# Four-network GNN kernel on one Trainium2 core: where ScalarE issues its transfers of P in the edge MLP of network L1

## The chip, the core and the metric

The kernel runs on one NeuronCore of a Trainium2 chip, as one launch. The metric is the device time of the launch in microseconds (us). The program uses all five instruction streams of the core: TensorE (PE), VectorE (DVE), ScalarE (ACT), GpSimd (POOL) and SyncE (SP). ScalarE and SyncE both issue direct DMA transfers, GpSimd issues indirect ones (gathers).

## The reference

Four small graph networks run one after another on 3125 nodes with 16 features and 103125 edges; each adds its output to `x` and normalises. The change lies in the second, L1, which has four layers with 128 hidden features. One layer is, cut to the part that matters:

```python
for i in range(L):                                   # L = 4
    ef = jnp.concatenate([h[row], h[col], edge_attr], axis=1)
    ef = jax.nn.silu(ef @ edge_w1[i] + edge_b1[i])
    ef = jax.nn.silu(ef @ edge_w2[i] + edge_b2[i])
    ef = ef * edge_mask
    agg = jax.ops.segment_sum(ef, row, num_segments=n)
    ...                                              # node MLP, h = h + nf
```

So every edge needs a row of `h` for its one end, a row for its other end, a two-layer MLP with silu, and a sum over the edges of a node.

## The kernel before

The first product of the edge MLP is split: per layer, `P = h @ w1[0:128]` and `Q = h @ w1[128:256]` are worked out for all nodes and written to the tables `p_tab` (three bf16 parts of 128 values each, 768 bytes a row) and `q_tab` (f32) in HBM. The edges lie sorted in 840 tiles of 128 edges. Three tiles are a group (M3 = 3), so a layer has G3 = 280 groups of 384 edges. `edge_mlp` (from line 1436) runs them; it is called once per layer, four times in all.

Every engine runs its own list of steps, one step per group, and the lists are tied by counting semaphores. `turns` (line 927) makes the list: eight steps, one for each slot h = 0 to 7 of the ring buffers (U3 = 8), are a turn; K3 = 35 turns are a layer, of which the first two and the last are written out and the 32 between are a loop. In the step of group n:

- TensorE: `first` (lines 1523 to 1531) adds up z1 of group n in PSUM: edge features (L1523), nine bf16 products of the P rows in `pb` with a one-hot matrix `oht` (L1526), in three groups of four a product of `qb` (L1528), and two or three transposes of the gathered Q rows `qg` (L1531). Then `sums` (L1549) adds the messages of group n-2 to the node sums; it waits for `m_seed`. Then `second` (L1540) multiplies h1 of group n-1 by w2 into z2.
- ScalarE: `two` (L1595), the silu of z2 of group n-2, which waits for `m_z2`; then `one` (L1588), the silu of z1 of group n, which waits for `m_z1`; and in even steps `fetch`, below.
- VectorE: `seed` (L1622) writes the bias b2 over z2, once `two` has read it, and so releases `sums` and `second`; then one-hot matrices (L1632, L1633, L1641) and the indices for the gathers (L1617).
- GpSimd: two or three gathers of Q rows (L1480) for a group five steps on.
- SyncE: in even steps all that a pair of groups needs besides: places, near, edge features, `qb`, and the three transfers of P rows of the even group (L1503).

There is only one z2 in PSUM. So `second` of a group can't start before `seed` has followed `two` of the group before it, and `two` can't start before `second` has ended.

ScalarE's `fetch(k, h)` is called at the end of even steps for the pair six steps on. It waits on `m_z1` for its ring slot, loads four numbers from `at_p` into registers (`address`, line 961, a TENSOR_LOAD), and issues three transfers of 96 KB each (L1581) of P rows into `pb` for the pair's odd group. All of it stands in ScalarE's list between `one` of the even step and `two` of the odd step. Its transfers are first read by `first` seven steps later.

Of the kernel before, what the change touches and what calls it, by code (L numbers as in the profile page):

```python
# [13 lines left out]
P = 128  # L14
N, FIN = 3125, 16
E = 103125
NB = -(-N // P)
# [8 lines left out]
M3 = 3  # L26
U3 = 8
# [27 lines left out]
def gnn_kernel(nc, a, out):  # L55

    with ExitStack() as ctx:
        def sb(name, shape, dt=F32, st=None):
            return (st or ctx).enter_context(nc.sbuf_tensor(name, shape, dt))

        def dram(name, shape, dt=F32):
            return nc.dram_tensor(name, shape, dt, kind="Internal").ap()

        def sem(name):
            return ctx.enter_context(nc.semaphore(name))
# [43 lines left out]
        p_tab = dram("p_tab", [NP, 3 * HID], BF16)  # L109
# [455 lines left out]
        at_p = sb("at_p", [1, G3, 4], I32)  # L565
# [361 lines left out]
        def turns(eng, step, rounds=K, ring=U):  # L927

            for k in (0, 1):
                for h in range(ring):  # L930
                    step(k, h)
            with eng.Fori(2, rounds - 1) as k:
                for h in range(ring):
                    step(k, h)
            for h in range(ring):
                step(rounds - 1, h)
# [24 lines left out]
        def address(eng, row, top):  # L961

            _, at = nc.values_load_multi_w_load_instructions(
                row, engines=[eng], min_val=0, max_val=top,
                skip_runtime_bounds_check_because="worked out on the chip from counts that are bounded by the shapes")
            return at
# [391 lines left out]
        with ExitStack() as st:  # L1358
# [5 lines left out]
            h = sb("h", [P, NB, FIN], F32, st)  # L1364
# [67 lines left out]
        m_pl, m_sp, m_act = ([sem(f"m_{n}{q}") for q in range(U3 // 2)] for n in ("pl", "sp", "act"))  # L1432
        Z1, Z2 = 3584, NP

        def edge_mlp(layer, we36, w2, b1, b2):
# [4 lines left out]
            def here(k, h, lag=0):  # L1440
                return not isinstance(k, int) or lag <= k * U3 + h < G3
# [7 lines left out]
            def moved(k, h, by):  # L1449

                d, slot = divmod(h + by, U3)
                return (k + d if d else k), slot

            with ExitStack() as st:
                qidx = sb(f"qidx{layer}", [P, U3, M3], I32, st)
                qg = sb(f"qg{layer}", [P, U3, M3, HID], F32, st)
                pb = sb(f"pb{layer}", [P, U3, M3, 3 * HID], BF16, st)
# [11 lines left out]
                with nc.Block() as block:  # L1469
                    @block.gpsimd  # L1470
                    def _(pool):
                        def gather(k, h):
                            n = k * U3 + h
                            if here(k, h, U3):

                                pool.wait_ge(m_z1, g0 + n - U3 + 1)
                            pool.wait_ge(m_idx, g0 + n + 1)
                            pool_gate(pool)
                            for j in range(gathered(h)):
                                pool.indirect_dma_start(qg[:, h, j, :], None, q_tab,  # L1480
                                                        IndirectOffsetOnAxis(ap=qidx[:, h, j:j + 1], axis=0)).then_inc(m_got[h], 16)
                        turns(pool, gather, K3, U3)
# [87 lines left out]

                    @block.scalar
                    def _(act):
                        def fetch(k, h):
                            q, n = h // 2, k * U3 + h
                            if not here(k, h):
                                return
                            if here(k, h, U3):
                                act.wait_ge(m_z1, g0 + n - U3 + 2)
                            at = address(mybir.EngineType.Activation, at_p[0:1, bass.ds(n + 1, 1), 0:4].rearrange("a g j -> a (g j)"), (NB - 1) * P)
                            for j in range(M3):  # L1580
                                act.dma_start(pb[:, h + 1, j, :], p_tab[bass.ds(at[j], P), :]).then_inc(m_act[q], 16)  # L1581

                        def one(k, h):
                            n = k * U3 + h
                            if here(k, h, 2):
                                act.wait_ge(m_z2, g0 + n - 1)
                            act.wait_ge(m_z1, g0 + n + 1)
                            act.activation(h1[:, h % 2, :], z1, ACT.Silu, bias=b1).then_inc(m_h1, 1)  # L1588

                        def two(k, h):  # L1590
                            n = k * U3 + h
                            if here(k, h, 2):
                                act.wait_ge(m_sum, g0 + n - 1)
                            act.wait_ge(m_z2, g0 + n + 1)
                            act.activation(h2[:, h % 2, :, :], z2.rearrange("p (j f) -> p j f", j=M3), ACT.Silu).then_inc(m_h2, 1)  # L1595

                        def step(k, h):
                            if here(k, h, 2):
                                two(*moved(k, h, -2))
                            one(k, h)  # L1600
                            if h % 2 == 0:
                                fetch(*moved(k, h, 6))
                        for h in (0, 2, 4):
                            fetch(0, h)
                        turns(act, step, K3, U3)
                        two(K3 - 1, U3 - 2)
                        two(K3 - 1, U3 - 1)
# [376 lines left out]
```

## Time and profile before

| what | value |
|---|---|
| median of 3 runs | 8916.31 us (8913.84 to 8923.95) |
| the profiled execution's own time | 8926.24 us |
| its span in the trace | 8924.5 us |
| mean granted clock of TensorE over the span | 0.794 of full speed |
| busy: TensorE, weight loads, VectorE, ScalarE, GpSimd | 6479.8, 5299.9, 4955.1, 2834.7, 5094.9 us |

The profile gives the busy time of each engine, the span in slices with the granted clock and the DMA share, groups of instructions by source line with the idle time of the engine in front of them, the waits between engines, and a timeline. In the timeline the "ACTq" and "SPq" rows are the issuing of transfers by ScalarE and SyncE; they don't count as busy. The ends of matmuls are modelled. The four layers' edge MLPs lie in the trace at about 2364 to 3285, 3370 to 4282, 4367 to 5289 and 5373 to 6289 us.

### The profile page before, as it was taken

Reading aid. Unit: us, or ns where it says so; the run is one execution under the profiler, and the core shown is the slowest. Engines: PE = TensorE matmul, PEld = TensorE weight load, DVE = VectorE, ACT = ScalarE, POOL = GpSimd, SP = SyncE. Lnnn points to the kernel's source line nnn. Section 1 sums busy time; section 2 is a strip of 40 time slices with the busy share of each in tenths; the row PEclk is TensorE's granted clock in tenths of the full one; section 3 lists DMA queues with packets and bytes.
Section 4 is the critical chain, followed back from the end, with each engine's and each line's share of the span. In section 5 each row is a group of like instructions: output and inputs, shape, how many; then the busy total and the mean of one; then the engine's idle time right before and its main releaser. Section 6 shows DMA issues by size and latency. Waiting matters only on the chain. (4 is left out here: it accounts for less than half of the span.)

```text
span 8924.5 us, 233638 instructions
## 1 busy us (share of the span) xinstructions
PE 6479.8 (73%) x55142; PEld 5299.9 (59%) x55143; DVE 4955.1 (56%) x13861; ACT 2834.7 (32%) x8499; POOL 5094.9 (57%) x7138
## 2 busy tenths in 40 slices
PE   1222225767688878888788878888866666888998
PEld 1111114555477756777577756777455555787998
DVE  6333346867455545555455545555322222998999
ACT  1222203545233333333233333333133333222554
POOL 3777736756366646666366646666067776222554
PEclk8555555555799999999899999999655555999999
DMA  2000004434477757777577757777311000332232
GB/s 63 3 3 3 3 29 133 121 98 120 126 200 200 200 132 206 202 203 199 134 201 202 201 132 203 202 203 199 88 24 7 7 7 6 79 82 59 73 72 60
DMA packets 1320021, 1000.55 MB, mean 112 GB/s; under 512 B 479878, under 2 KB 1224219, under 8 KB 1319000
## 3 DMA queue, kind: packets, MB, share of 16 engines
q1 hardware_dynamic: 942230, 649.30, 26.7%
q0 software_dynamic: 134272, 178.98, 10.4%
q10 hardware_dynamic: 243392, 170.76, 6.6%
q8 instruction: 57, 0.93, 0.0%
q14 instruction: 70, 0.57, 0.0%
HBM read 951.88 MB, written 54.19 MB: 113 GB/s over the span
## 5 line engine op out<-in xcount | busy, mean ns | idle before, releaser
L1480 POOL DMA_INDIRECT qg<-q_tab,qidx x2520 | 2390.0, 948 | 1376.2 <-issue 769.9
L1622 DVE COPY ps<-b 128x384 f32<-128x384 f32 x1120 | 627.9, 561 | 1693.5 <-ACT h L1595 1655.3
L1067 PE MATMUL ps<-rhs_i,ohi 128*128 128x128 f32 (+2 forms) x8640 | 1216.7, 267 | 209.1 <-issue 197.1
L1549 PE MATMUL ps<-ohm,h 128*128 128x128 f32 x6720 | 1034.1, 291 | 380.7 <-DVE ps L1622 371.4
L1067 PEld LDWEIGHTS ps<-rhs_i,ohi 128*128 128x128 f32 (+1 forms) x8640 | 1000.4, 163 | 339.1 <-issue 280.6
L1549 PEld LDWEIGHTS ps<-ohm,h 128*128 128x128 f32 x6720 | 839.3, 192 | 592.0 <-issue 591.7
L1595 ACT ACTIVATE h<-ps 128x384 f32<-128x384 f32 x1120 | 549.2, 490 | 1824.7 <-PE ps L1540 1744.8
L1033 POOL COPY near<-x 128x48 bf16 x2160 | 675.4, 351 | 790.7 <-PE ps L1056 433.8
L1195 POOL DMA_INDIRECT got_m<-y_tab,idx_m x832 | 813.1, 977 | 473.5 <-issue 252.3
L375 POOL DMA_INDIRECT list_by_src<-ring,rpos x808 | 782.9, 969 | 348.9 <-issue 255.0
L1212 PE MATMUL ps<-rhs_m,ohi_m 128*128 x2880 | 668.8, 403 | 413.1 <-ACT rhs_m L1238 387.7
L1641 DVE TENSOR_SCALAR ohm<-iota_row,loc_p,w_p 128x128 f32<-128x128 f32 x3360 | 961.1, 358 | 0.0
L1540 PE MATMUL ps<-w,h 128*128 128x128 f32 x6720 | 943.4, 277 | 0.0
L1128 DVE TENSOR_TENSOR ohi<-iota_row,dst_i 128x512 f32<-128x512 f32 (+1 forms) x1080 | 930.5, 862 | 0.0
L1212 PEld LDWEIGHTS ps<-rhs_m,ohi_m 128*128 128x128 f32 x2880 | 637.0, 328 | 445.7 <-issue 445.5
L1588 ACT ACTIVATE h<-ps,b 128x384 f32<-128x384 f32 x1120 | 650.1, 580 | 707.5 <-PE ps L1531 666.4
L1540 PEld LDWEIGHTS ps<-w,h 128*128 128x128 f32 x6720 | 850.3, 194 | 0.0
L1526 PE MATMUL ps<-oht,pb 128*128 128x128 bf16 x10080 | 766.2, 222 | 0.0
L1252 DVE TENSOR_TENSOR ohi_m<-iota_row,dst_i 128x512 f32<-128x512 f32 x360 | 249.3, 693 | 831.3 <-PE ps L1212 827.3
L1526 PEld LDWEIGHTS ps<-oht,pb 128*128 128x128 bf16 x10080 | 572.3, 98 | 197.1 <-issue 197.1
L1123 DVE TENSOR_SCALAR oht_i<-places_i,iota_p 128x512 bf16<-128x512 bf16 (+1 forms) x1080 | 512.8, 475 | 177.8 <-PE ps L1067 160.2
L1031 POOL COPY near<-z 128x384 bf16 x720 | 344.8, 508 | 366.8 <-PE ps L1056 305.0
(443 smaller groups left out, 8613.0 us busy)
## 6 DMA issues: line engine op xcount, KB each, us to landing
pb<-p_tab ACTq DMA_DIRECT2D x1680, 96.0 KB
pb<-p_tab SPq DMA_DIRECT2D x1680, 96.0 KB
places<-place_by_turn SPq DMA_DIRECT2D x560, 192.0 KB
places_i<-place_by_meeting SPq DMA_DIRECT2D x360, 256.0 KB, 3.4
places_i<-place_by_meeting SPq DMA_DIRECT2D x720, 128.0 KB, 3.1
qb<-q_tab SPq DMA_DIRECT2D x840, 64.0 KB
qg<-q_tab,qidx POOLq DMA_INDIRECT x2520
nears<-near_by_turn SPq DMA_DIRECT2D x560, 64.0 KB
```

The source lines that it names most:

```text
L375: pool.indirect_dma_start(list_s[:, :], IndirectOffsetOnAxis(ap=rpos[:, h, c:c + 1], axis=0), ring[:, h, c, :], None).then_inc(scattered[h ...
L1033: m = pool.tensor_copy(near[:, h, j, :], table[:, bass.ds(at[j], 48)])
L1067: m = pe.matmul(ps[:, bass.ds(to[j], width)], ohi[:, h, j, :], rhs[:, h, j, 0:width], start=False, stop=True, skip_group_check=True)
L1128: dve.tensor_tensor(ohi[:, h, :, :], iota_row[:, None, :].to_broadcast([P, M, P]), dst_i[:, bass.ds(n * M, M)][:, :, None].to_broadcast([P ...
L1195: pool.indirect_dma_start(got[:, h, j, :], None, y_tab, IndirectOffsetOnAxis(ap=idx[:, h, j:j + 1], axis=0)).then_inc(d_got[h], 16)
L1212: m = pe.matmul(ps[:, bass.ds(to[j], 32)], ohi[:, h, j, :], rhs[:, bass.ds(at[j], 1), :].rearrange("p t f -> p (t f)"), start=False, stop= ...
L1480: pool.indirect_dma_start(qg[:, h, j, :], None, q_tab, IndirectOffsetOnAxis(ap=qidx[:, h, j:j + 1], axis=0)).then_inc(m_got[h], 16)
L1526: pe.matmul(z1[:, j * P:(j + 1) * P], pb[:, h, j, q_ * HID:(q_ + 1) * HID], oht[:, h, j * P:(j + 1) * P], start=False, stop=False)
L1540: m = pe.matmul(z2[:, j * P:(j + 1) * P], h1[:, h % 2, j * P:(j + 1) * P], w2, start=False, stop=True, skip_group_check=True)
L1549: m = pe.matmul(ps[:, bass.ds(to[M3 * (h % 2) + j], P)], h2[:, h % 2, j, :], ohm[:, h % 2, j, :], start=False, stop=True, skip_group_check ...
L1588: act.activation(h1[:, h % 2, :], z1, ACT.Silu, bias=b1).then_inc(m_h1, 1)
L1641: m = dve.tensor_scalar(ohm[:, h % 2, j, :], iota_row[:, :], loc_p[:, bass.ds(t, 1)], w_p[:, bass.ds(t, 1)], ALU.is_equal, ALU.mult)
```

## The change

`fetch` is cut in two: `find(k, h)` waits for the ring slot and loads the four numbers; `fetch(k, h, j)` issues one of the three transfers. In an even step `find` now stands between `two` and `one`, and transfer 0 behind `one`. In the odd step that follows, transfer 1 stands between `two` and `one`, and transfer 2 behind `one`. The three fetches ahead of the first step stay as they were.

```diff
-                        def fetch(k, h):
-                            q, n = h // 2, k * U3 + h
+                        at = []
+
+                        def find(k, h):
+                            n = k * U3 + h
                             if not here(k, h):
                                 return
                             if here(k, h, U3):
                                 act.wait_ge(m_z1, g0 + n - U3 + 2)
-                            at = address(mybir.EngineType.Activation, at_p[0:1, bass.ds(n + 1, 1), 0:4].rearrange("a g j -> a (g j)"), (NB - 1) * P)
-                            for j in range(M3):
-                                act.dma_start(pb[:, h + 1, j, :], p_tab[bass.ds(at[j], P), :]).then_inc(m_act[q], 16)
+                            at[:] = address(mybir.EngineType.Activation, at_p[0:1, bass.ds(n + 1, 1), 0:4].rearrange("a g j -> a (g j)"), (NB - 1) * P)
+
+                        def fetch(k, h, j):
+                            if not here(k, h):
+                                return
+                            act.dma_start(pb[:, h + 1, j, :], p_tab[bass.ds(at[j], P), :]).then_inc(m_act[h // 2], 16)
...
                         def step(k, h):
                             if here(k, h, 2):
                                 two(*moved(k, h, -2))
+                            if h % 2 == 0:
+                                find(*moved(k, h, 6))
+                            else:
+                                fetch(*moved(k, h, 5), 1)
                             one(k, h)
                             if h % 2 == 0:
-                                fetch(*moved(k, h, 6))
+                                fetch(*moved(k, h, 6), 0)
+                            else:
+                                fetch(*moved(k, h, 5), 2)
                         for h in (0, 2, 4):
-                            fetch(0, h)
+                            find(0, h)
+                            for j in range(M3):
+                                fetch(0, h, j)
```

On ScalarE, inside the loop of a layer, a pair of steps before (L1595 is `two`, L1588 is `one`, the TENSOR_LOAD is the address load, ISA and REGISTER_ALU are its sequencer's register work):

```order
L1595 ACTIVATE h<-ps 128x384 [waits m_z2,m_sum]
L1587 REGISTER_ALU [waits m_z2]
L1588 ACTIVATE h<-ps,b 128x384 [waits m_z1]
L1578 ISA
L963 ISA [waits m_z1]
L963 TENSOR_LOAD at_p
L1581 ISA
L1581 DMA pb<-p_tab 128x384
L1581 ISA
L1581 DMA pb<-p_tab 128x384
L1581 ISA
L1581 DMA pb<-p_tab 128x384
```

Here one load and three transfers stand in a row between `one` and the next `two`. The same place after the change (L1600 is `two`, L1593 is `one`, L1586 the transfers):

```order
L1600 ACTIVATE h<-ps 128x384 [waits m_z2,m_sum]
L1580 ISA
L963 ISA [waits m_z1]
L963 TENSOR_LOAD at_p
L1592 REGISTER_ALU [waits m_z2]
L1593 ACTIVATE h<-ps,b 128x384 [waits m_z1]
L1586 ISA
L1586 DMA pb<-p_tab 128x384
```

and the odd step behind it:

```order
L1600 ACTIVATE h<-ps 128x384 [waits m_z2,m_sum]
L1586 ISA
L1586 DMA pb<-p_tab 128x384
L1592 REGISTER_ALU [waits m_z2]
L1593 ACTIVATE h<-ps,b 128x384 [waits m_z1]
L1586 ISA
L1586 DMA pb<-p_tab 128x384
```

In front of each `two` and each `one` there is now at most one transfer or one load. The instructions of TensorE, VectorE, GpSimd and SyncE and their waits stand in the same order as before.

## Rows read from the trace of the kernel before

**Rows 1.** Groups by line over the whole span: busy, mean ns, idle before.
```profile
L1549 PE MATMUL ps<-ohm,h 128*128 128x128 f32 x6720 | 1034.1, 291 | 380.7 <-DVE ps L1622 371.4
```

**Rows 2.** Waits in 3400 to 4200 us: total us, times, longest.
```profile
DVE ps L1622 <- ACT h L1595: 357.3, 248, 2.2
...
POOL qg L1480 <- DVE qidx L1617: 101.6, 78, 2.0
...
PE ps L1549 <- DVE ps L1622: 72.4, 124, 0.9
```

**Rows 3.** Timeline, first matmul of each group in a turn of layer 1: start, length.
```profile
3500.90 0.33 PE L1523 MATMUL ps<-eat,we 36*128 36x384 bf16 x1 [0.34 <-issue]
...
3503.61 0.33 PE L1523 MATMUL ps<-eat,we 36*128 36x384 bf16 x1
...
3507.28 0.33 PE L1523 MATMUL ps<-eat,we 36*128 36x384 bf16 x1
...
3510.19 0.33 PE L1523 MATMUL ps<-eat,we 36*128 36x384 bf16 x1
...
3513.60 0.33 PE L1523 MATMUL ps<-eat,we 36*128 36x384 bf16 x1
...
3519.91 0.33 PE L1523 MATMUL ps<-eat,we 36*128 36x384 bf16 x1
...
3522.83 0.33 PE L1523 MATMUL ps<-eat,we 36*128 36x384 bf16 x1
...
3526.58 0.33 PE L1523 MATMUL ps<-eat,we 36*128 36x384 bf16 x1 [0.31 <-issue]
```

**Rows 4.** Timeline of slots 2 and 3 of that turn, ScalarE and what it releases.
```profile
3507.44 0.49 ACT L1595 ACTIVATE h<-ps 128x384 f32<-128x384 f32 x1 [1.78 <-PE ps L1540]
...
3507.96 0.56 DVE L1622 COPY ps<-b 128x384 f32<-128x384 f32 x1 [1.10 <-ACT h L1595]
...
3508.66 0.93 PE L1549 MATMUL ps<-ohm,h 128*128 128x128 f32 x6
...
3508.75 0.58 ACT L1588 ACTIVATE h<-ps,b 128x384 f32<-128x384 f32 x1 [0.82 <-PE ps L1531]
...
3509.41 1.33 ACTq L1581 DMA_DIRECT2D pb<-p_tab  x3
3509.42 0.83 PE L1540 MATMUL ps<-w,h 128*128 128x128 f32 x6
...
3510.85 0.49 ACT L1595 ACTIVATE h<-ps 128x384 f32<-128x384 f32 x1 [1.52 <-PE ps L1540]
...
3511.37 0.56 DVE L1622 COPY ps<-b 128x384 f32<-128x384 f32 x1 [1.79 <-ACT h L1595]
3511.50 0.58 ACT L1588 ACTIVATE h<-ps,b 128x384 f32<-128x384 f32 x1 [0.16 <-PE ps L1531]
...
3512.07 0.93 PE L1549 MATMUL ps<-ohm,h 128*128 128x128 f32 x6 [0.60 <-DVE ps L1622]
```

**Rows 5.** Timeline ahead of layer 0: nine transfers and three loads in a row.
```profile
2355.66 5.22 ACTq L1581 DMA_DIRECT2D pb<-p_tab  x9
```

**Rows 6.** Timeline, first matmul of three groups in layer 0.
```profile
2814.76 0.33 PE L1523 MATMUL ps<-eat,we 36*128 36x384 bf16 x1
...
2817.78 0.33 PE L1523 MATMUL ps<-eat,we 36*128 36x384 bf16 x1
...
2821.20 0.33 PE L1523 MATMUL ps<-eat,we 36*128 36x384 bf16 x1
```

**Rows 7.** Timeline of GpSimd, a gather in an unbroken row of them.
```profile
3562.26 0.94 POOL L1480 DMA_INDIRECT qg<-q_tab,qidx  x1 [0.30 <-issue]
```

**Rows 8.** Two stretches: busy of each engine, granted clock, DMA share, GB/s.
```profile
3500.00:4100.00 600.00, 537.63 (x4807) 447.46 (x4806) 330.76 (x1258) 199.62 (x373) 398.00 (x419) 1.00 0.75 202
3366.00:3376.00 10.00, 3.92 (x25) 2.87 (x25) 2.83 (x12) 0.58 (x1) 7.56 (x9) 0.62 1.04 275
```

## Prediction

> **What bounds the kernel now.** I began with the groups by line. In the whole span TensorE sat idle for 380.7 us in front of L1549, `sums`, and 371.4 us of that ended with VectorE's L1622, `seed` [rows 1]. The waits of layer 1 give the link behind it: `seed` in turn waited 248 times for ScalarE's L1595, `two`, and TensorE waited 124 times for `seed`, 72.4 us in 800 us [rows 2]. There are some 249 groups in that stretch, so only every second group makes TensorE wait. No wait on a transfer stands in the list.
>
> The timeline says which. The first matmuls of the groups of one turn [rows 3] start 2.71, 3.67, 2.91, 3.41 us after one another in slots 0 to 3; the pair of slots 4 and 5 takes 6.31, slot 6 takes 2.92 and slot 7 takes 3.75, with the 0.31 us of TensorE's loop end in it. The turn is 25.68 us. Even steps are short, odd steps long. In the even slot 2 [rows 4] ScalarE starts `one` at 3508.75. Its three issues then take it from 3509.41 to 3510.74. Meanwhile `second` ends on TensorE at 3509.42 + 0.83 = 3510.25. `two` starts at 3510.85, right behind the issues, and not at 3510.35, where it would follow `second` as closely as it does elsewhere (0.10 us). `seed` is late with it, and `sums` stalls 0.60 us. One step before, with no issue in front of it, `two` started at 3507.44 and `sums` had no idle time at all. So the path that sets the end here is `second`, `two`, `seed`, `sums`, `second`, through four engines' queues, and ScalarE's issues lie on it once a pair.
>
> **What the freed path would take.** From rows 4: `sums` to `second` 0.76 us (3508.66 to 3509.42), `second` 0.83, to `two` 0.10, to `seed` 0.52 (3510.85 to 3511.37), `seed` 0.56, to `sums` 0.14. That is 2.91 us, the length of slots 2 and 6 [rows 3]. The chain, not TensorE's own work, already sets the even steps; TensorE's own work for a group is the 2.71 us of slot 0, which has the loop end in front of it as a cushion.
>
> **The change, part by part.**
> *Removed from behind `one` of the even step:* the load and two of three issues. An issue is 1.33 / 3 = 0.44 us [rows 4]. The batch held ScalarE from 3508.75 to 3510.85, 2.10 us; with one issue instead of three that is 2.10 - 0.89 = 1.21 us, even if the load's share stayed in it. `two` is needed 1.60 us after the start of `one` (3508.75 to 3510.35). So transfer 0 is hidden by TensorE's `second`, with 0.39 us to spare, and the lateness of 0.50 us goes.
> *Added between `two` and `one` of the even step:* wait and load. The wait is for a z1 that TensorE finished a step earlier, so it costs nothing. The load: nine issues and the two loads between them took 5.22 us [rows 5], so a load is at most (5.22 - 9 x 0.44) / 2 = 0.63 us; the lower bound is nothing. From `two` at 3507.44 to `one` at 3508.75 there are 1.31 us, and `two` itself takes 0.49 [rows 4]. 0.49 + 0.63 = 1.12 fits. If this cover were gone, `one` would slip, and nobody needs h1 before the next group's `first`, at 3510.19, while `one` ended at 3509.33: another 0.86 us of slack. I take nothing.
> *Added between `two` and `one` of the odd step:* transfer 1. `two` 0.49, a gap as before the issues now of under 0.10, 0.44 for the issue, and 0.11 until ScalarE starts the next activation (3510.74 to 3510.85): 1.14 of 1.31 us. Nothing.
> *Added behind `one` of the odd step:* transfer 2, 1.21 us of 1.60 as above. Nothing. At slot 7 ScalarE's branch comes on top, but there `sums` of slot 0 has the loop end's cushion.
> *The transfers themselves:* the same 288 KB in the same queue, the last of them issued about one step (3 us) later than before. They are read seven steps on, some 20 us, so they don't come late by that. SyncE's and GpSimd's lists are untouched.
>
> **The sum.** Every odd step falls to the chain's 2.91: slot 1 saves 3.67 - 2.91 = 0.76, slot 3 saves 3.41 - 2.91 = 0.50, slot 5 saves 6.31 - 2 x 2.91 = 0.49. Slot 7 keeps its loop end; I take 0.45, a little under the others. 2.20 us a turn, 25.68 to 23.5. Layers 1 to 3 look alike: 105 turns, 231 us. In layer 0 a plain step takes 3.02 us and a pair 6.44 [rows 6], so a pair saves 0.40; four pairs, 35 turns, 56 us. Together 287 us. The profiled execution took 8926.24 us, so 8639 for one like it; it lies 10 us above the median of 8916.31, from which 287 us gives **8629 us**. A difference of 0.2% (18 us) is about what a measurement of this kernel can tell from none.
>
> The bounds: if all layers fall to 23.4 to 23.5 and the starts and ends of layers gain too, the saving nears the 371.4 us less what slots 3 and 7 keep (about 0.1 us each, since their `first` is shorter than the chain; 28 us), 340 us: 8575; I don't think the starts gain, so 8588 is the low end. If every layer's chain is as slow as layer 0's, 140 x 1.6 = 224 us: 8692.
>
> **A rule against it.** The issue of three transfers holds ScalarE 1.33 us, and `two` is late by 0.50 for it [rows 4]. The Trainium skill, "DMA: Bandwidth & Descriptors", section "Issuing engines are not separate DMA queues", says that issuing from several engines saves only the sequencer's time for it, and calls that usually small beside the transfer. By that rule there is little to win by moving an issue. The trace disagrees here, since the sequencer's time lies in front of an activation on the path.
>
> **The rivals.**
> *A, GpSimd becomes the bound.* A turn has 18 gathers, each 0.94 + 0.30 us apart when nothing holds them [rows 7]: 22.3 us, against 23.5 forecast. It fits, by 5%; it waits for VectorE's indices now, 101.6 us in 800 [rows 2], so it has slack. But should each of the eight groups add 0.2 us between its gathers, it would need 24.0; then the gain is 1.7 x 140 less layer 0's share, some 225 us: 8690. Chance 0.08.
> *B, the transfers come late.* The DMA share is 0.75 at 202 GB/s [rows 8]. At 23.5 us a turn it would be 0.82 at 221 GB/s. Against: the engines moved 275 GB/s at the start of layer 1 [rows 8], and nothing waits for a transfer now. For: near a full share queues grow. If half the gain went to this: 8916 - 143 = 8773. Chance 0.09.
> *C, no change.* Either `two` was late for another reason than the issues, with 0.11 us between the two a coincidence, or the issue time is as small as the skill's rule has it. It stays at 8916. Chance 0.04.
> *D, slower: a lone issue costs ScalarE nearly what three do.* The place is behind `one`, in every step now and not in every second. If the 2.10 us that ScalarE was held were set-up and not number, `two` would be 0.50 late in all eight steps of a turn: 4.0 us, where now 2.2 are lost. 1.8 x 140 = 250 us more: 9166. It decides from a hold of 1.60 us on, and the kernel gets slower from about 1.88 us. Against it: nine issues took 5.22 us and three 1.33, so the price goes with the number. Chance 0.04.
>
> **How the numbers follow.** The forecast has the rest, 0.75. The range from 8588 to 8700 takes in the forecast's bounds and rival A; B, C and D, 0.17 together, are left out. Faster by over 0.2%: the forecast, A and B, 0.92. Same: C, 0.04. Slower: D, 0.04.
>
> **What would show it.** In the profile after, the first matmuls of layer 1 should stand 2.9 us apart in odd and even steps alike, a turn at 23.5 us; `two` should start 0.1 us behind the end of `second` in every step; TensorE's idle time in front of `sums` should fall from 380.7 us to under 90. The wait of `one` for z1 should stay, as the sign that load and transfer 1 fit in front of it. GpSimd's wait for the indices should shrink to near 1 us a turn, and the DMA share rise to 0.82. The prediction is wrong if `two` starts right behind an issue in any slot (D), if the gathers run without a wait for indices while TensorE waits for them at L1531 (A), or if TensorE waits for transfers (B).

## The result

The changed kernel takes 8633.99 us (median of 4 runs, 8630.37 to 8649.17), the kernel before 8916.33 us in the same comparison: a ratio of 0.9685, 95% interval 0.9668 to 0.9702, 282 us less. The forecast was 8629 us.

| what | before | after |
|---|---|---|
| the profiled execution's own time | 8926.24 us | 8636.00 us |
| its span | 8924.5 us | 8634.3 us |
| busy: TensorE, VectorE, ScalarE, GpSimd | 6479.8, 4955.1, 2834.7, 5094.9 us | 6448.2, 4984.1, 2837.3, 5094.3 us |
| mean granted clock over the span | 0.794 | 0.787 |

### The profile after

The same work is done (the busy times are alike) in 290 us less. The page's groups by line, as in [rows 1]; L1635 is `seed` in the changed kernel:

```profile
L1549 PE MATMUL ps<-ohm,h 128*128 128x128 f32 x6720 | 1033.9, 291 | 61.4 <-DVE ps L1635 30.9
```

TensorE's idle time in front of `sums` fell from 380.7 us [rows 1] to 61.4, and what ended on `seed` from 371.4 to 30.9. That is 319 us, more than the gain, since other idle time of TensorE grew: in front of L1523, the first matmul of a group, from 68.2 to 108.4 us, and in front of L1531, which reads the gathered rows, from nothing to 17.2 us, all of it ended by a gather's landing. What was added lies in the last turns of the layers, shown below.

The waits of 3350 to 4100 us, to be read against [rows 2]:

```profile
ACT h L1593 <- PE ps L1531: 200.2, 238, 1.3
...
POOL qg L1480 <- DVE qidx L1630: 46.4, 98, 2.0
```

TensorE's wait for `seed` is down to one of 0.2 us in this stretch. `one` (L1593) waits for z1 in nearly every step: ScalarE is early there, behind the load and behind transfer 1 alike.

The first matmuls of one turn of layer 1, the counterpart of [rows 3]:

```profile
3427.52 0.33 PE L1523 MATMUL ps<-eat,we 36*128 36x384 bf16 x1 [0.35 <-issue]
...
3430.22 0.33 PE L1523 MATMUL ps<-eat,we 36*128 36x384 bf16 x1
...
3433.08 0.33 PE L1523 MATMUL ps<-eat,we 36*128 36x384 bf16 x1
...
3435.99 0.33 PE L1523 MATMUL ps<-eat,we 36*128 36x384 bf16 x1
...
3438.90 0.33 PE L1523 MATMUL ps<-eat,we 36*128 36x384 bf16 x1
...
3447.64 0.33 PE L1523 MATMUL ps<-eat,we 36*128 36x384 bf16 x1
...
3450.96 0.33 PE L1523 MATMUL ps<-eat,we 36*128 36x384 bf16 x1 [0.34 <-issue]
```

The steps are 2.70, 2.86, 2.91, 2.91 us; the three from 3438.90 to 3447.64 take 8.74, 2.91 each; slot 7 takes 3.32. The turn is 23.44 us, against 25.68 [rows 3]. Odd and even steps are alike.

Slots 0 and 1 of that turn, ScalarE and what it releases, to be read beside [rows 4]. L1600 is `two`, L1593 `one`, L1586 a transfer:

```profile
3428.99 0.58 ACT L1593 ACTIVATE h<-ps,b 128x384 f32<-128x384 f32 x1 [1.29 <-PE ps L1531]
3429.12 0.37 ACTq L1586 DMA_DIRECT2D pb<-p_tab  x1
...
3429.46 0.83 PE L1540 MATMUL ps<-w,h 128*128 128x128 f32 x6
...
3430.33 0.49 ACT L1600 ACTIVATE h<-ps 128x384 f32<-128x384 f32 x1 [0.76 <-PE ps L1540]
3430.46 0.34 ACTq L1586 DMA_DIRECT2D pb<-p_tab  x1
...
3430.85 0.56 DVE L1635 COPY ps<-b 128x384 f32<-128x384 f32 x1 [1.21 <-ACT h L1600]
...
3431.54 0.93 PE L1549 MATMUL ps<-ohm,h 128*128 128x128 f32 x6
```

`two` starts at 3430.33, 0.04 us behind the modelled end of `second` (3429.46 + 0.83), where for the odd step of [rows 4] it came 0.60 us behind that end. A lone issue starts 0.13 us after the start of an activation, while that activation still runs, and takes 0.34 to 0.37 us. The issuing (not the transfer itself) is over before the activation in front of it has ended.

The stretch in the middle of layer 1, against [rows 8]:

```profile
3450.00:4050.00 600.00, 586.05 (x5276) 491.34 (x5275) 368.39 (x1384) 219.20 (x410) 437.95 (x463) 1.00 0.82 222
```

DMA share and rate are 0.82 and 222 GB/s, and TensorE is granted its full clock (2.4 GHz) as before.

The ends of the layers look different. Of the last turns of layer 0, changed kernel (L1493 is a transfer that SyncE issues):

```profile
3189.94 3.52 SPq L1493 DMA_DIRECT2D places<-place_by_turn  x1
...
3197.17 0.90 PE L1531 MATMUL ps<-ident,qg 128*128 128x128 f32 x3 [3.03 <-DMA qg<-q_tab,qidx]
...
3209.30 0.47 PE L1523 MATMUL ps<-eat,we 36*128 36x384 bf16 x1 [8.71 <-issue]
```

and the busy time by stretch there, of the changed kernel and then of the kernel before at the same place:

```profile
3190.00:3200.00 10.00, 5.75 (x38) 5.05 (x38) 3.37 (x12) 2.14 (x4) 3.04 (x4) 0.85 1.00 78
```

```profile
3250.00:3260.00 10.00, 6.54 (x49) 5.46 (x48) 3.49 (x14) 1.58 (x4) 3.91 (x5) 0.83 0.97 111
```

In both kernels the DMA engines are busy all the time there and move 78 and 111 GB/s, against 222 and 202 in the middle of a layer; an issue of SyncE takes up to 3.5 us in place of 0.34, and the granted clock falls. In the changed kernel TensorE waits 3.03 us for a gather and then stands idle for 8.71 us, during which SyncE issues its transfers of P. The other layers have one such stop each, of 9.02, 9.85 and 11.13 us, where the kernel before has none. The last turn (seven steps between its first matmuls) is 10 to 13 us longer than before in each layer, and the turn ahead of it 6 to 9 us shorter. What makes the transfers slow there is not shown; in the stretch above, the packets of the gathers' queue take 85% of the DMA engines' time.

### The profile page after: what moved, and what is told of

It reads as the page before. It is cut to its first block and busy times, and to the rows that moved or that the text cites. A ratio compares the mean times of both kernels' runs of the same rounds, so it can differ in the third digit from the quotient of the medians.

```text
span 8634.3 us, 233670 instructions
## 1 busy us (share of the span) xinstructions
PE 6448.2 (75%) x55142; PEld 5295.3 (61%) x55143; DVE 4984.1 (58%) x13861; ACT 2837.3 (33%) x8499; POOL 5094.3 (59%) x7138
## 3 DMA queue, kind: packets, MB, share of 16 engines
q0 software_dynamic: 134272, 178.98, 10.6%
## 5 line engine op out<-in xcount | busy, mean ns | idle before, releaser
L1635 DVE COPY ps<-b 128x384 f32<-128x384 f32 x1120 | 628.1, 561 | 1386.5 <-ACT h L1600 1376.6
L1549 PE MATMUL ps<-ohm,h 128*128 128x128 f32 x6720 | 1033.9, 291 | 61.4 <-DVE ps L1635 30.9
L1593 ACT ACTIVATE h<-ps,b 128x384 f32<-128x384 f32 x1120 | 650.2, 581 | 1064.8 <-PE ps L1531 981.8
L1600 ACT ACTIVATE h<-ps 128x384 f32<-128x384 f32 x1120 | 548.9, 490 | 1181.2 <-PE ps L1540 1122.2
```

What stands on the lines that cost most here:

```text
L1549: m = pe.matmul(ps[:, bass.ds(to[M3 * (h % 2) + j], P)], h2[:, h % 2, j, :], ohm[:, h % 2, j, :], start=False, stop=True, skip_group_check ...
```

## Experiments

**Theory 1, the path:** the loss before was `two` of the odd step coming late, by as long as ScalarE was held beyond 1.60 us after the start of `one`; whatever shortens that hold gives the gain. **Its rival, the spread:** it is the row of three transfers that has to be broken up. **Theory 2** came from a reading of the trace, that layer 0's steps are 0.11 us longer than those of the other layers.

All runs but those marked _b were on a second chip, where every kernel, the one before too, takes 10.6 to 10.9 ms. What that chip does is told at the end; from its traces I use single steps between its stops (for a slot, the length that its undisturbed turns have, which is the lower quartile of its steps). The runs marked _b are on chips where the kernel before takes its 8920 us.

### Only the load moved (load_only, load_only_b)

```diff
                             if h % 2 == 0:
                                 find(*moved(k, h, 6))
-                            else:
-                                fetch(*moved(k, h, 5), 1)
                             one(k, h)
                             if h % 2 == 0:
-                                fetch(*moved(k, h, 6), 0)
-                            else:
-                                fetch(*moved(k, h, 5), 2)
+                                for j in range(M3):
+                                    fetch(*moved(k, h, 6), j)
```

> Only the address load moves, to between the two activations of the even step; the three issues stay in a row behind the even step's second activation. Theory 1 (the path): two is late by as long as ScalarE is held beyond 1.60 us after the start of one, whatever holds it. In the changed kernel an issue starts 0.13 us after the start of one when no load is in front of it, and a row of three takes 1.33 us: 0.13 + 1.33 + 0.11 = 1.57 us, just inside. So nearly the whole gain comes from the load alone: a turn of 23.4 to 23.7 us, 8634 to 8670 us. Rival (the spread): three transfers in a row are what has to be broken up, and the time stays within 0.5% of 8916 us.

Measured on the second chip: ratio 0.9925 (0.9898 to 0.9953), 10589.81 us against 10675.03. With that chip's stops in it this decides little.

> The same kernel as load_only. On the chip of the first two calls every kernel, the one before too, took 10.6 to 10.9 ms, with engines that stand idle for 2 to 4 us at fixed places of a turn; there its odd steps took 3.0 to 3.1 us (slots 1 and 5), against 2.85 and 2.91 in the changed kernel and 3.67 and 3.40 in the one before. On a chip without those stops theory 1 expects a turn of 23.44 us + 4 x 0.05 to 0.2 us: 8640 to 8745 us; the rival (the spread) 8916 us.

Measured: 8684.47 us against 8921.51, ratio 0.973 (0.9714 to 0.9747), 237 us less. That is inside the second expectation, and 14 us past the upper end of the first. The load alone gives five sixths of the gain. Two stretches of its timeline (L1632 is `seed`), a plain pair and the start of a turn:

```profile
3452.20 0.58 ACT L1593 ACTIVATE h<-ps,b 128x384 f32<-128x384 f32 x1 [0.82 <-PE ps L1531]
3452.34 1.34 ACTq L1586 DMA_DIRECT2D pb<-p_tab  x3
...
3452.87 0.83 PE L1540 MATMUL ps<-w,h 128*128 128x128 f32 x6
...
3453.80 0.49 ACT L1600 ACTIVATE h<-ps 128x384 f32<-128x384 f32 x1 [1.02 <-PE ps L1540]
...
3470.16 0.58 ACT L1593 ACTIVATE h<-ps,b 128x384 f32<-128x384 f32 x1 [1.31 <-PE ps L1531]
3470.29 1.36 ACTq L1586 DMA_DIRECT2D pb<-p_tab  x3
...
3470.63 0.83 PE L1540 MATMUL ps<-w,h 128*128 128x128 f32 x6
...
3471.84 0.49 ACT L1600 ACTIVATE h<-ps 128x384 f32<-128x384 f32 x1 [1.10 <-PE ps L1540]
```

Three issues in a row, 1.34 us, start at once behind the start of `one` and are over at 3453.68; `two` comes at 3453.80, 0.10 behind the end of `second`. The rival is out: nothing has to be spread. Only in slot 0, where `second` comes early, does the row reach past it: z2 is there at 3471.46, the issues end at 3471.65, `two` starts at 3471.84, 0.28 late. That is once a turn, 39 us in 140 turns (an estimate, 0.28 x 140), of the 45 by which this kernel misses the full gain. The steps say the same: slot 1 of layer 1 has a median of 3.20 us here and 2.85 in the changed kernel, and the other slots are nearly alike.

### Only the issues spread (issues_only, issues_only_b)

```diff
-                            if h % 2 == 0:
-                                find(*moved(k, h, 6))
-                            else:
+                            if h % 2:
                                 fetch(*moved(k, h, 5), 1)
                             one(k, h)
                             if h % 2 == 0:
+                                find(*moved(k, h, 6))
                                 fetch(*moved(k, h, 6), 0)
```

> Only the three issues are spread as in the change; the load stays behind one in the even step, ahead of transfer 0. Theory 1: ScalarE is held 0.64 + 0.37 + 0.11 = 1.12 us after the start of one, inside 1.60: the whole gain, a turn of 23.4 us in layers 1 to 3, 8630 to 8645 us. Rival (the load is what costs, since the registers' use has to wait for it): some of the lateness of 0.50 us stays, and the time lies between 8700 and 8916 us.

Measured on the second chip: ratio 0.9897 (0.9852 to 0.9941), two runs.

> The same kernel as issues_only. On the chip with the stops its slots 1 and 5 took 2.85 and 2.91 us as in the changed kernel. Without stops theory 1 expects the changed kernel's time, 8630 to 8645 us. Rival (the load matters by itself): 8684 us or more, as with the load alone moved.

Measured: 8646.27 us against 8924.71, ratio 0.9687 (0.9672 to 0.9702), the changed kernel's ratio, though 1 us past the expected range. Its rows:

```profile
3452.31 0.58 ACT L1593 ACTIVATE h<-ps,b 128x384 f32<-128x384 f32 x1 [0.82 <-PE ps L1531]
3452.94 0.38 ACTq L1586 DMA_DIRECT2D pb<-p_tab  x1
3452.98 0.83 PE L1540 MATMUL ps<-w,h 128*128 128x128 f32 x6
...
3453.91 0.49 ACT L1600 ACTIVATE h<-ps 128x384 f32<-128x384 f32 x1 [1.02 <-PE ps L1540]
```

With the load in front the issue starts 0.63 us after `one`, without it 0.13: a load costs 0.50 us of ScalarE's issuing here. The issue ends at 3453.32, half a microsecond before `two` is due. So moving the load is worth nothing once the issues are spread; either half of the change nearly does.

### Load and issues in a row, in front of `one` (ahead)

```diff
                             if h % 2 == 0:
                                 find(*moved(k, h, 6))
-                            else:
-                                fetch(*moved(k, h, 5), 1)
+                                for j in range(M3):
+                                    fetch(*moved(k, h, 6), j)
                             one(k, h)
-                            if h % 2 == 0:
-                                fetch(*moved(k, h, 6), 0)
-                            else:
-                                fetch(*moved(k, h, 5), 2)
```

> Load and all three issues move in a row to between two and one of the even step. Theory 1: two of the odd step is on time; one of the even step starts at about 0.17 + 0.64 + 1.33 + 0.11 = 2.25 us after the group's first matmul in place of 1.47, and ends at 2.83, just ahead of the next group's first matmul at 2.91. So it costs nothing or up to 0.05 us a pair: 8630 to 8665 us. Rival (the spread): a row of three holds back an activation wherever it stands, so the lateness of 0.78 us of one shows in full, and the time is 8900 us or more.

It ran on the second chip only: ratio 0.9919 (0.9887 to 0.9952), beside 0.992 for the changed kernel there. A pair between two stops (L1631 is `seed`):

```profile
4535.43 0.50 PE L1523 MATMUL ps<-eat,we 36*128 36x384 bf16 x1
4535.59 0.49 ACT L1600 ACTIVATE h<-ps 128x384 f32<-128x384 f32 x1 [2.04 <-issue]
...
4536.23 1.34 ACTq L1586 DMA_DIRECT2D pb<-p_tab  x3
...
4537.69 0.58 ACT L1593 ACTIVATE h<-ps,b 128x384 f32<-128x384 f32 x1 [1.62 <-PE ps L1531]
4538.34 0.33 PE L1523 MATMUL ps<-eat,we 36*128 36x384 bf16 x1
```

`one` is held back to 2.26 us after the step's first matmul (1.47 is usual) and ends at 4538.27. The next first matmul comes at 4538.34, the step is 2.91 us, nothing is lost. In this step the row stands where the activation has slack. What a whole run of this kernel takes on a chip without stops was not tried.

### Two more issues on the path (before_plus2, before_plus2_b)

```diff
+                spare = sb(f"spare{layer}", [P, U3 // 2, 2, 8], BF16, st)
...
-                                pe.wait_ge(m_act[q], 48 * (k0 + k + 1))
+                                pe.wait_ge(m_act[q], 80 * (k0 + k + 1))
...
                             for j in range(M3):
                                 act.dma_start(pb[:, h + 1, j, :], p_tab[bass.ds(at[j], P), :]).then_inc(m_act[q], 16)
+                            for j in range(2):
+                                act.dma_start(spare[:, q, j, :], p_tab[bass.ds(at[j], P), 0:8]).then_inc(m_act[q], 16)
```

> The kernel before, with two more small transfers (128 rows of 16 bytes) issued behind the three, into a tile that nobody reads. Theory 1: each issue is 0.44 us more on the path in every odd step: 4 x 0.88 = 3.5 us a turn, 140 turns, some 490 us: 9350 to 9450 us. Rival (ScalarE's hold is set-up and not number, or the path lies elsewhere): under 9100 us.

Measured on the second chip: ratio 1.0191 (1.0141 to 1.0242), 10877.08 us against 10675.03, two runs.

> The same kernel as before_plus2. On the chip with the stops its slots 1 and 5 took 4.2 to 4.5 and 4.1 to 4.5 us, against 3.67 and 3.40 in the kernel before on a chip without them. Theory 1: each issue adds 0.44 us or a little more to every odd step: 9350 to 9500 us. Rival (the lateness is soaked up elsewhere): under 9200 us.

Measured: 9581.91 us against 8924.71, ratio 1.0732 (1.0716 to 1.0749), 657 us more, past the upper end. The rows (L1591 is `one`, L1598 `two`, L1584 the two extra issues, L1625 `seed`, L1550 `sums`):

```profile
3625.16 0.58 ACT L1591 ACTIVATE h<-ps,b 128x384 f32<-128x384 f32 x1 [0.82 <-PE ps L1532]
3625.79 1.33 ACTq L1582 DMA_DIRECT2D pb<-p_tab  x3
3625.83 0.83 PE L1541 MATMUL ps<-w,h 128*128 128x128 f32 x6
...
3627.21 0.88 ACTq L1584 DMA_DIRECT2D spare<-p_tab  x2
...
3628.19 0.49 ACT L1598 ACTIVATE h<-ps 128x384 f32<-128x384 f32 x1 [2.45 <-PE ps L1532]
...
3629.40 0.93 PE L1550 MATMUL ps<-ohm,h 128*128 128x128 f32 x6 [1.53 <-DVE ps L1625]
```

An extra transfer of 2 KB holds ScalarE 0.44 us, just as one of 96 KB does, plus 0.09 us in front of the two. The odd steps of layer 1 became 4.64, 4.42, 4.34 and 4.75 us (medians over the loop's turns), some 0.96 us longer than before in each: 3.84 us a turn, 538 us in 140 turns. So the path is confirmed by its slope. The other 119 us show in a second stretch of the same timeline, where TensorE comes out of a longer stall:

```profile
3604.73 1.41 PE L1550 MATMUL ps<-ohm,h 128*128 128x128 f32 x6 [2.28 <-DVE ps L1625]
...
3605.94 1.49 PE L1541 MATMUL ps<-w,h 128*128 128x128 f32 x6
```

and in the busy time by stretch of the same kernel (PE, PEld, DVE, ACT, POOL and so on, the granted clock, DMA's share, GB/s):

```profile
3500.00:4100.00 600.00, 464.52 (x3824) 378.98 (x3823) 285.05 (x1095) 159.93 (x342) 323.40 (x348) 0.94 0.67 173
```

`second` takes 1.49 us there and not 0.83, and the mean granted clock of the stretch is 0.94, not 1.00: from 3605 to 3608 us, after TensorE has stood idle for 2.28 us, the granted clock is 0.50 (1.2 GHz), and such falls come in most turns of this layer. Turns of layer 1 without one have a median of 29.55 us, which is the old turn and the 3.84, and turns with one 31.08. In the kernel before and the changed one the granted clock is 1.00 throughout the stretches shown of layer 1; in the edge MLPs of both it falls only at the starts and ends of layers.

### The same two issues off the path (after_plus2, after_again)

```diff
                             act.dma_start(pb[:, h + 1, j, :], p_tab[bass.ds(at[j], P), :]).then_inc(m_act[h // 2], 16)
+                            if j == 0:
+                                for i in range(2):
+                                    act.dma_start(spare[:, h // 2, i, :], p_tab[bass.ds(at[i], P), 0:8]).then_inc(m_act[h // 2], 16)
```

The tile `spare` and TensorE's wait for 80 are as in before_plus2.

> The changed kernel, with the same two more small transfers as before_plus2, behind transfer 0 in the even step. Theory 1: ScalarE is held 0.13 + 3 x 0.44 + 0.11 = 1.56 us after the start of one, inside 1.60, so the same extra issues that cost the kernel before some 490 us cost nothing here: 8630 to 8670 us. Rival (issues cost wherever they stand): 8850 us or more.

> The changed kernel unchanged, as the measure for the others of this call: 8634 us within 0.2%.

Both were measured on the second chip, so neither figure expected for a chip without stops was met or refuted: 10736.06 us with the two extra issues and 10734.96 without, ratios to the kernel before 0.9921 (0.9904 to 0.9937) and 0.992 (0.9903 to 0.9938). The same two transfers that cost the kernel before 1.9% on that chip cost the changed one nothing that can be told. In the steps it is not quite nothing: undisturbed steps of slots 1 and 5 of layer 1 take 3.15 and 3.07 us there, and 2.85 and 2.91 without; the row reaches past `second` by a little, as it does in load_only_b. On a chip without stops this kernel was not tried.

### The form of a wait (waits_swapped, waits_swapped_b, ohm_early)

In layer 0 `sums` starts later behind `seed` than in the other layers. Of the changed kernel, layer 0 first, `seed` and `sums`, then `first`:

```profile
2802.49 0.56 DVE L1635 COPY ps<-b 128x384 f32<-128x384 f32 x1 [0.98 <-ACT h L1600]
...
2803.29 0.93 PE L1549 MATMUL ps<-ohm,h 128*128 128x128 f32 x6
2804.82 0.33 PE L1523 MATMUL ps<-eat,we 36*128 36x384 bf16 x1
```

From the end of `seed` (2803.05) to `sums` 0.24 us; in layer 1 above 3431.54 - 3431.41 = 0.13. TensorE's list differs there in form. In layer 0's loop the wait for `m_seed`, the late one, is an instruction of its own (it runs at 2803.09), and a register instruction with the wait for `m_ohm` still follows it (2803.20) ahead of the weight load (2803.28). In the other layers the wait for `m_ohm` is passed earlier, and that for `m_seed` rides on the last register instruction (3431.45), with the weight load next (3431.54). The expectation below has the two semaphores of layer 0 the other way round.

```diff
-                            pe.wait_ge(m_ohm, g0 + n + 1)
                             pe.wait_ge(m_seed, s0 + 3 + n)
+                            pe.wait_ge(m_ohm, g0 + n + 1)
```

> The changed kernel with the two waits of sums on TensorE in the other order: m_seed first, then m_ohm. In layer 0 sums starts 0.24 us after the end of seed and in layers 1 to 3 0.14 us; in layer 0's loop the wait for m_ohm is an instruction of its own, in the others it rides on a register instruction. Theory 2 (the form of the wait makes the 0.1 us): with the other order all four layers have the same form, and all have the same plain step, 2.91 or 3.02 us: 8610 or 8710 us. Rival (layer 0's data or tables make it): layer 0 keeps 3.02, the others 2.91, 8634 us.

Measured on the second chip: 10776.63 us, ratio 0.9953 (0.9936 to 0.9969), a little slower than the changed kernel beside it (10734.96), while the step in question did fall, slot 5 of layer 0 from 3.02 to 2.91 us where it is undisturbed.

> The same kernel as waits_swapped. On the chip with the stops, layer 0's slot 5 took 2.91 us with the swapped waits and 3.02 with the old order, so the form of the wait makes the 0.1 us. On a chip without stops: layer 0's turn falls from 24.12 to 23.44 us, 35 turns, 24 us: 8600 to 8615 us, the best so far. Rival (one plain step more or less is lost elsewhere in the turn): 8634 us.

Measured: 8616.2 us against 8924.71, ratio 0.9654 (0.9641 to 0.9667). Beside it on the same chip issues_only_b, which has the changed kernel's ratio, took 8646.27. It is the fastest of all, 1 us past the expected range. Layer 0 of this kernel:

```profile
2802.83 0.56 DVE L1635 COPY ps<-b 128x384 f32<-128x384 f32 x1 [1.07 <-ACT h L1600]
...
2803.52 0.93 PE L1549 MATMUL ps<-ohm,h 128*128 128x128 f32 x6
2805.06 0.33 PE L1523 MATMUL ps<-eat,we 36*128 36x384 bf16 x1
...
2807.97 0.33 PE L1523 MATMUL ps<-eat,we 36*128 36x384 bf16 x1
```

0.13 us from `seed` to `sums`, and 2.91 us a step. Layer 0 as a whole, from its first group to its last, takes 838.7 us and not 859.2. Theory 2 holds for layer 0: the 0.11 us are the step from the wait to the register instruction that stood behind it (2803.09 to 2803.20). The third form, with the wait for `m_ohm` moved ahead of `first`:

```diff
-                            pe.wait_ge(m_ohm, g0 + n + 1)
                             pe.wait_ge(m_seed, s0 + 3 + n)
...
+                            if here(k, h, 2):
+                                pe.wait_ge(m_ohm, g0 + k * U3 + h - 1)
                             first(k, h)
...
```

> The changed kernel with the wait for m_ohm moved from sums to ahead of first of the same step, where it has long been fulfilled; sums then waits for m_seed alone, in all layers. Theory 2: layer 0's plain step falls from 3.02 to 2.91 us, its turn from 24.1 to 23.4: 8605 to 8615 us. If the register instruction between the waits is what helps layers 1 to 3, they could lose 0.1 us a step: up to 8720 us. Rival (layer 0's data): 8634 us.

It ran on the second chip only: ratio 0.9946 (0.9929 to 0.9963), with undisturbed steps of slot 5 at 2.91 us in all four layers. The step is repaired, and the time there is inconclusive, as for waits_swapped.

## Why the prediction was right

- *The path.* That ScalarE's `two` sets the odd steps, through `seed`, held: with the hold shortened the stall went, and with two more issues it grew by 0.96 us a step. (The path runs through the queues of three engines, TensorE, ScalarE and VectorE, not of four as the prediction says.)
- *The chain at 2.91 us.* Slots 2 to 6 came out at 2.91 us, slot 7 at 3.32 (3.30 forecast), slot 1 at 2.86, a little less, because `sums` of slot 0 is not late and `second` follows it 0.67 us on, not 0.76. The turn is 23.44 us; 23.5 was forecast.
- *Layer 0.* Its plain step stayed at 3.02 us, as taken. Its loop turns have a median of 24.12 us (26.04 before), 1.92 us saved a turn where the sum had 1.6: it took one pair for all four, and slot 1 fell from 3.59 to 2.85 us.
- *The sum.* 287 us forecast, 290 us between the two profiled executions, 282 between the medians. That it is so close is partly luck. From first group to last the four layers save 60, 70, 80 and 74 us, 284 in all. In the 30 turns of a layer from the fourth to the 33rd they save 267 us where the sum has 246; in the first three turns and the last two they save 17 us where it has 41. It took the ends of the layers to be like the middle, and there TensorE is held up by late gathers and late issues.
- *Load and transfers cost nothing where they stand.* This held: in layer 1's loop the odd steps have the chain's length. But the sizes were off, all on the safe side: a lone issue ends 0.50 us after the start of `one`, not 1.21 us, since it starts during the activation; and the load is 0.50 us, not 0.63. In the batch the load was the part that made it late. The price list of the prediction would have allowed a smaller edit: its own 2.10 - 0.63 = 1.47 lies inside 1.60, and load_only_b, which is that edit, saves 237 us.
- *Rival A, GpSimd.* It kept up. It waits for indices 46.4 us in 750, 1.45 us a turn, so its gathers would fit in some 22 us. *Rival B, late transfers:* in the middle of a layer none waits at 222 GB/s. At the ends of layers its sign did appear, in the 17.2 us of waits for gathers in front of L1531, which had none before, and in the stops of 8.71 to 11.13 us above, 38.7 us in the four layers. The last two turns of the layers together take 16 us more than before, so this is far from half the gain, but it is what a next change could look at. *Rival C* and the rule behind it are out: issuing is not small here, 1.33 us for three transfers whose size hardly matters. *Rival D* is out: a lone issue takes 0.34 to 0.37 us, three 1.33, and two more lengthened the odd steps by 0.96.

The Trainium skill, "DMA: Bandwidth & Descriptors", section "Latency and other measured facts", gives a floor of about 600 ns for a tensor_load. The runs here show 0.50 us from it between the start of an activation and the first issue behind it, so somewhat less shows on the queue.

## What to carry to other kernels

Look at what an engine issues between two of its compute instructions, and take the time from the start of the earlier one to when the later one's input is ready; issues and register loads are free inside that window and cost their full time past it, here 0.44 us an issue and 0.50 us a load. A window that has slack can take them in a row; to spread them matters only where no window is long enough. And an edit's gain can be capped by the next chain: here `second`, `two`, `seed`, `sums` at 2.91 us a step is what is left, with TensorE's own 2.70 just below it.

## What was not expected of the hardware

- *An issue does not wait for the activation in front of it.* It starts 0.13 us after the activation's start and runs beside it.
- *Chips differ.* On the second chip the kernel before took 10675 us the first time and 10823 us the second, and the change gave 0.992 (0.9903 to 0.9938), not 0.9685. The changed kernel there:

```profile
3708.44 0.58 ACT L1593 ACTIVATE h<-ps,b 128x384 f32<-128x384 f32 x1 [2.60 <-issue]
...
3712.16 0.49 ACT L1600 ACTIVATE h<-ps 128x384 f32<-128x384 f32 x1 [3.14 <-remote]
...
3713.49 1.19 PE L1549 MATMUL ps<-ohm,h 128*128 128x128 f32 x6 [3.07 <-DVE ps L1635]
```

  The busy time by stretch of the same kernel, its last three columns the granted clock, DMA's share and GB/s:

```profile
3500.00:4100.00 600.00, 435.58 (x3099) 348.69 (x3099) 242.29 (x905) 146.87 (x301) 252.60 (x273) 0.83 0.53 135
```

  ScalarE stands idle for 3.14 us although z2 was ready at 3708.28, and the profile names nothing on the core that it waited for ("remote", "issue"). Single instructions take what they take elsewhere (0.49, 0.58 us). Such stops come at the same places of the turns: layer 1's slots 0, 2, 3, 6 and 7 have medians of 3.6 to 6.5 us in the changed kernel, slots 1 and 5 keep 2.9. The granted clock of the stretch is 0.83. There is no trace of the kernel before from that chip; that it has the same stops, and that they take up part of what the odd steps save, is inferred from its time alone. What makes them is open: no run here took away what an engine might be waiting for.
- *An idle TensorE costs twice.* Stalls of about 0.6 us a pair left the granted clock at 1.00. With stalls of 1.5 to 2.3 us it was 0.94 over the stretch, and the kernel lost 119 us more than the steps' own lengthening.
- *The form of a double wait.* Where the late wait stands first, with a register instruction for the other wait behind it, TensorE starts 0.11 us later than where the late wait stands last.
